# Four DRAM reads of an attention kernel move from SyncE's queue to ACT's

## The reference: what is computed

```python
h = _L0_tok_ref(x, ...)
h = h + _L0_attn_ref(_layernorm(h), ...)    # scores, softmax, attn @ v, @ Wo
h = h + _L0_ffn_ref(_layernorm(h), ...)     # gelu(h @ in + b) @ out
```

## Time and profile before

| | before |
|---|---|
| median of 3 runs | 995.44 us (994.3 to 996.88) |
| the profiled execution, its own time | 997.25 us |
| its span in the trace | 995.3 us |
| granted clock of TensorE, mean | 0.997 |
| busy: TensorE, weight loads, VectorE, ACT, POOL | 97%, 84%, 82%, 68%, 66% |
| DMA, mean over the span | 125 GB/s |
| period of a steady step | 29.7 us |

### The profile page before, as it was taken

One profiled execution on the slowest core, in us unless ns is written; L12 is line 12 of the kernel. 1 busy time (PEld: TensorE's weight loads), 2 busy tenths in 40 slices (PEclk: granted clock), 3 DMA queues, 4 the chain that ended last, 5 costly groups with the idle time before them and its releaser, 6 DMA issues.

```text
span 995.3 us, 25836 instructions
## 1 busy us (share of the span) xinstructions
PE 962.2 (97%) x7402; PEld 831.5 (84%) x7402; DVE 815.3 (82%) x1996; ACT 679.5 (68%) x2469; POOL 655.9 (66%) x936
## 2 busy tenths in 40 slices
PE   6889999999999999999999999999999999999988
PEld 4778888888888898888898888898888898888877
DVE  3788788888888888888888888888888888888862
ACT  3656677667677667777667777667777666767653
POOL 2777566777666777666767666767666767666671
PEclk9999999999999999999999999999999999999999
DMA  6053454444554444554444545444545444545331
GB/s 192 23 143 104 124 154 121 122 120 123 142 148 124 123 123 117 150 140 134 114 132 108 155 135 140 112 133 109 149 134 145 113 132 116 137 134 149 97 109 24
DMA packets 193600, 124.54 MB, mean 125 GB/s; under 512 B 31153, under 2 KB 185137, under 8 KB 193585
## 3 DMA queue, kind: packets, MB, share of 16 engines
q1 hardware_dynamic: 190720, 121.04, 44.4%
q10 hardware_dynamic: 2864, 3.33, 1.0%
HBM read 69.26 MB, written 55.05 MB: 125 GB/s over the span
## 4 chain that ended last, share of the span: by engine, by line
PE 65%; DMA 16%; DVE 6%; SPq 6%; issue 3%; POOL 2%; ACT 1%; DVEq 0%; ACTq 0%; POOLq 0%
PE ring L821 14%; PE ring L1034 13%; PE ring L892 8%; DMA spill<-EB 8%; DMA ET<-spill 8%; PE ring L799 6%; SPq L252 5%; PE ring L859 5%; PE bank L840 4%; PE ring L960 3%; DVE EB L580 2%; PE ring L967 2%; PE bank L967 2%; PE bank L1001 2%; PE ring L956 1%
## 5 line engine op out<-in xcount | busy, mean ns | idle before, releaser
L320 ACT ACTIVATE E<-ring,m_neg 128x128 f32<-128x128 f32 x768 | 273.1, 380 | 19.4 <-DVE m_neg L566 18.3
L455 POOL TENSOR_TENSOR qkT<-rot_c,rot_s 128x256 f32<-128x256 f32 x256 | 187.3, 731 | 20.1
L463 POOL TENSOR_TENSOR E<-E,e_rcp 128x512 f32<-128x512 f32 x158 | 175.1, 1124 | 36.0 <-DVE e_rcp L589 36.0
L320 ACT ACTIVATION_READ_ACCUMULATOR E<-ring,m_neg 128x1 f32 x768 | 167.0, 217 | 0.0
L453 POOL TENSOR_TENSOR rot_s<-rot_s,rope_qs 128x256 f32<-128x256 f32 x192 | 146.5, 763 | 2.8 <-DVE rot_s L554 2.3
L840 PE MATMUL bank<-wout_sb,G 128*128 128x192 f32 x744 | 141.1, 326 | 0.0
L566 DVE TENSOR_REDUCE m_neg<-ring 128x4 f32<-128x512 f32 x192 | 129.9, 678 | 9.8 <-PE ring L859 9.8
L580 DVE STREAM_TRANSPOSE EB<-E 128x512 f32<-128x512 f32 x186 | 124.8, 686 | 15.1 <-POOL E L463 15.1
L1034 PE MATMUL ring<-wo_sb,OT 128*128 128x192 f32 x744 | 134.3, 331 | 0.6 <-DVE OT L611 0.6
L1034 PEld LDWEIGHTS ring<-wo_sb,OT 128*128 128x128 f32 x744 | 120.3, 191 | 7.2 <-issue 7.2
L840 PEld LDWEIGHTS bank<-wout_sb,G 128*128 128x128 f32 x744 | 119.7, 190 | 0.4 <-issue 0.4
(11 more groups left out here) (159 smaller groups left out, 2487.8 us busy)
## 6 DMA issues: line engine op xcount, KB each, us to landing
spill<-EB SPq DMA_DIRECT2D x186, 256.0 KB, 2.3
ET<-spill SPq DMA_DIRECT2D x248, 128.0 KB, 2.7
ET<-spill SPq DMA_DIRECT2D x248, 64.0 KB, 2.3
x_sb<-in_x_dram SPq DMA_DIRECT2D x64, 192.0 KB, 2.5
out_dram<-out_sb SPq DMA_DIRECT2D x64, 96.0 KB, 2.3
x_sb<-in_x_dram SPq DMA_DIRECT2D x64, 64.0 KB, 2.4
w_raw<-in_w_att_dram ACTq DMA_DIRECT2D x2, 608.0 KB, 4.5
win_raw<-in_w_in_dram ACTq DMA_DIRECT2D x2, 384.0 KB, 5.8
```

Source lines behind the costliest of these rows:

```text
L320: last = nc.scalar.activation(E[:, a, s * P:(s + 1) * P], RING[a][:, s * P:(s + 1) * P], ACT.Exp, bias=m_neg[:, a, s:s + 1], accum_out=e_s ...
L455: nc.gpsimd.tensor_tensor(qkT[:, b, :, a], rot_c[:, b, :, a], rot_s[:, b, :, a], ALU.add).then_inc(q_out, 1)
L463: nc.gpsimd.tensor_tensor(e, e, r, ALU.mult).then_inc(prob_out, 1)
```

## The change

The four reads of the second piece are taken out of SyncE's `blocks_moved` for a = 0 (not for a = 1) and are issued through ACT's queue, after the first of the three exp groups of a = 1 and ahead of the other two. The two waits go along: for `pv_mm`, and for the landed spill of group 2. Semaphores, addresses and sizes stay as they are. It holds in each step with attention but p = 0, where the first sequence's blocks don't go through DRAM.

```diff
--- before.py
+++ after.py
@@ -243,7 +243,7 @@
-                for k, (s0, heads) in enumerate(PIECES):
+                for k, (s0, heads) in enumerate(PIECES if a == 1 else PIECES[:1]):
                     c = slice(s0 * P, (s0 + heads) * P)
                     need(sp, pv_mm, 4 * (q - 1) + 2 * a + k + 1)
                     for m in ((0, 1), (2,))[k]:
@@ -402,8 +402,17 @@
                 elif att:
-                    for k in range(NKV):
-                        score_exp(1, k)
+                    score_exp(1, 0)
+                    s0, heads = PIECES[1]
+                    c = slice(s0 * P, (s0 + heads) * P)
+                    act.wait_ge(pv_mm, 4 * p - 2)
+                    act.wait_ge(spilled[2], 32 * p + 16)
+                    for j in range(NB):
+                        act.dma_start(ET[j * B32:(j + 1) * B32, 0, c].rearrange("r (i e) -> r i e", i=NB),
+                                      spill[0, :, c].rearrange("(i r) (j e) -> j r i e", i=NB, j=NB)[j]
+                                      ).then_inc(filled[1], 16)
+                    score_exp(1, 1)
+                    score_exp(1, 2)
                     heads_out(p)
```

## The result

The changed kernel takes 1011.7 us (median of 4 runs, 1009.96 to 1014.22) against 994.91 us (median of 4, 994.3 to 996.88) for the kernel before on the same chip: a ratio of 1.0156, with a 95% interval of 1.0137 to 1.0175. It is slower by 16.8 us. The forecast was slower by 9.3 us, 1004.7, with a range up to 1013.

The account below looks back on a forecast made before the run. TensorE was 97% busy, with DMA engines pacing the first piece's reads. First piece 0.6 us later, 0.30 us wait gone: +0.30 us a step, +9.3 us in 31 steps, 1004.7 us against the 995.44 median; range 988 to 1013.

Parts of the forecast that it names:

- What bounds the block: TensorE's probs_v block waits for ET reads, 0.15 and 0.30 us a step; DMA engines, not SyncE, pace the first piece.
- When the reads are issued: ACT, ahead of its engine, issues the four reads from 520.45, done about 522.2; second piece issued 1.25 us sooner.
- The rival that ACT's queue does not run ahead: ACT issues only after the first exp group, 521.4; -0.3 to +0.3 us a step, 986 to 1005 us; chance 0.08.
- What is queued on ACT, cost zero: Second exp group starts at 522.3 rather than 521.83; first OT copy's wait for TensorE covers it; uncovered, up to 0.4 us.
- What is gained, 0.30 us a step: The wait ahead of and in the second probs_v product goes, 0.30 us a step over 31 steps.
- the faster rival: Issue was the limit: first piece delayed under 0.2 us, second piece's wait gone, 9.3 us gained, 986.1 us; chance 0.24.
- What is lost, 0.6 us: First piece's last read lands later behind two second-piece reads at 0.3 us each: 0.6 us a step (0.4 to 1.0).
- The rule of the Trainium skill: DMA engines alternate between queues: three or four reads ahead of first piece's last, 0.9 to 1.3 us, total 1014 to 1026.
- The prologue's rows: SyncE's x_sb loads beside ACT's weight reads land in 3.9 us against median 2.5; the late queue waited, rates not adding.
- The store beside the second piece, without cost: SyncE's earlier result store may delay the second piece's last landing 0.3 us; nothing lost while first piece is later.

Follow-up runs that it names:

- the split: Against the kernel before: SyncE issues reads 0 and 1 of both pieces, ACT reads 2 and 3, first piece first in each queue; 993.1 us, ratio 0.9988.
- xn sooner: Both pieces' reads divided over SyncE and ACT, plus VectorE taking the next pair's layer-norm statistics before HL, against the kernel before; 985.25 us, ratio 0.99.
- the held half: Against the changed kernel: only two second-piece reads on ACT, held until SyncE has issued the first piece's four; other two on SyncE; 993.74 us, 0.9995.

## Why the prediction was right, and where its sizes were off

- **What bounds the block**: right. The DMA engines set the pace of the first piece; the first piece's wait took the place of the second's, and the block's growth alone (16.2 us) is about the loss (16.8 us).
- **When the reads are issued**: right to 0.02 us. The first came 0.62 us after SyncE's first, where 0.64 was expected (520.45 - 519.81), under running exps. The rival that ACT's queue does not run ahead is out.
- **What is queued on ACT, cost zero**: right. The second group moved by 0.47 us, and a hold of 0.85 us alone gives 1.0001.
- **What is gained, 0.30 us a step**: right in the changed kernel (0.30 to zero). For the faster rival it was too much: the split removed both waits and gained 1.1 us, since with xn late the gain was given back; with xn sooner 985.25 us were measured. I named no next wait, though the rival's 986.1 us rested on one being absent.
- **What is lost, 0.6 us**: the term that was mis-sized; it measured 0.82 us (0.97 - 0.15), inside its bounds of 0.4 to 1.0. Two reads ahead at 0.3 us each were sound (0.54 us for two). The step that failed is the count: the third and fourth read were priced at nothing in the sum because they are issued after the first piece's last. They cost 0.15 us, by the held half more likely the third than the fourth; the rest, about 0.1 us, is the store or chance. So the time came out near the top of the range (1011.7 of 1013).
- **The rule of the Trainium skill** (DMA: Bandwidth & Descriptors, Queues, rings and completion order), that DMA engines take turns between queues, gave an estimate of 0.9 to 1.3 us; the 0.82 us lie between it and mine. The prologue's rows, for which I stayed at 0.6, were no guide to the size; why was not tried.
- **The store beside the second piece, without cost**: right for the change, where the first piece is the later one. In the kernel with the reads one group later that cover was gone, and I had not carried the condition into its expectation; there the second wait grew to 1.03 us, though the store's share of it is not shown.

## What to carry to other kernels

Here a second queue brought the issues forward far more than the landings: in the change all eight reads were issued 1.3 us sooner and landed no sooner, in the split 1.8 us sooner and landed 0.4 us sooner. Before moving a read, look at whether the time to landing grows along the burst, and if so ask which read the consumer needs first and keep all others behind it in both queues. Four 64 KB reads let in among four 128 KB reads cost 1.6%; the same eight, split so that the first piece leads in each queue, cost nothing. Where a wait is removed without a gain, look for the next input of the same engine: here two changes worth 1.1 and 3.4 us alone gave 9.7 us together.

## What the runs showed of the hardware that was not expected

- Small reads are not cheap company: four reads of 4 KB on the other queue, each of 128 rows of 32 bytes, lengthened the landing of SyncE's 64 KB reads from 2.3 to 2.7 us up to 2.7 to 3.0 us and cost 1.29%, against 3.09% for four of 64 KB.
- Reads of the other queue can hold up a read that was issued just before them: 0.15 us for two, issued 0.14 and 0.6 us after it, by the first wait of four reads against two, both with the store held. Two issued 0.57 and 0.9 us after it did not (first wait 0.14 us, 0.15 before).
